# Five places instead of four for softmax probabilities, and inverted denominators written into the attention tile

## The reference, cut to what matters

```python
# L, H, NH, NKV, HD, FF, E, K = (4, 128, 16, 4, 64, 256, 8, 2); 2 rows, 1024 tokens
def _attention(x, wq, wk, wv, wo, cos, sin, causal_bias):
    q, k, v = ...                      # 16 query heads, 4 key/value heads of 64, rotary embedding on q and k
    scores = jnp.einsum('bhqd,bhkd->bhqk', q, k) / jnp.sqrt(jnp.asarray(HD, x.dtype))
    scores = scores + causal_bias
    attn = jax.nn.softmax(scores, axis=-1)
    out = jnp.einsum('bhqk,bhkd->bhqd', attn, v)
    return out.transpose(0, 2, 1, 3).reshape(b, s, NH * HD) @ wo
for l in range(L):
    x = clip(x + _attention(_rms(x, ln1_w[l]), ...), -100, 100)
    x = clip(x + _moe(_rms(x, ln2_w[l]), ...), -100, 100)
```

## Time and profile before

| | |
|---|---|
| runs | 3286.43, 3292.33, 3299.35 us; median 3292.33 |
| profiled execution | 3288.13 us, span of its instructions 3286.3 us |
| granted TensorE clock, mean | 0.98 |
| busy: TensorE, VectorE, ScalarE, GpSimd | 3080.0, 2606.2, 2173.4, 2014.8 us |

### The profile page before, as it was taken

One profiled execution on the slowest core, in us unless ns is written; L12 is line 12 of the kernel. 1 busy time (PEld: TensorE's weight loads), 2 busy tenths in 40 slices (PEclk: granted clock), 3 DMA queues, 4 the chain that ended last, 5 costly groups with the idle time before them and its releaser, 6 DMA issues. The chain is left out here.

```text
span 3286.3 us, 50731 instructions
## 1 busy us (share of the span) xinstructions
PE 3080.0 (94%) x16864; PEld 2042.4 (62%) x16864; DVE 2606.2 (79%) x3764; ACT 2173.4 (66%) x4011; POOL 2014.8 (61%) x1573
## 2 busy tenths in 40 slices
PE   5999999799999999999999999999999999999998
PEld 3555455456666577666665776666657766666576
DVE  6778776678888678888886778888867888888677
ACT  4566667576666676766666767666667676666675
POOL 2100000377878666778776757788767677877675
PEclk8899999899999999999999999999999999999999
DMA  5342421333223055323230653333215532332053
GB/s 121 75 76 49 87 57 38 80 74 81 67 68 75 24 190 146 88 64 77 68 74 16 193 147 83 71 71 76 63 26 190 151 88 66 76 71 66 23 185 112
DMA packets 160401, 283.55 MB, mean 86 GB/s; under 512 B 32592, under 2 KB 64208, under 8 KB 159888
## 3 DMA queue, kind: packets, MB, share of 16 engines
q1 hardware_dynamic: 159632, 280.18, 33.7%
q10 hardware_dynamic: 512, 0.13, 0.0%
HBM read 88.47 MB, written 31.72 MB: 37 GB/s over the span
## 5 line engine op out<-in xcount | busy, mean ns | idle before, releaser
L1473 ACT ACTIVATE prob<-psA 128x512 f32<-128x512 f32 x1152 | 657.6, 593 | 512.0 <-PE psA L1871 329.3
L1275 POOL TENSOR_TENSOR xw<-xw,prob 128x512 f32<-128x512 f32 x672 | 871.9, 1297 | 170.2 <-ACT prob L1473 103.1
L2195 DVE TENSOR_REDUCE mxp<-psA 128x1 f32<-128x512 f32 (+3 forms) x864 | 527.7, 663 | 60.3 <-PE psA L1840 59.6
L2169 DVE RECIPROCAL rden<-psA 128x256 f32<-128x256 f32 x256 | 448.6, 1752 | 151.6 <-PE psA L1899 149.0
L1870 PE MATMUL psA<-qs,ks 128*128 128x512 f32 x1152 | 505.0, 438 | 14.7 <-ACT prob L1473 7.9
L1840 PE MATMUL psA<-ks,qs 128*128 128x512 f32 (+3 forms) x1536 | 439.7, 369 | 40.3 <-DVE ks L2297 16.7
L1275 POOL TENSOR_TENSOR xw<-prob 128x512 f32<-128x512 f32 x224 | 288.2, 1287 | 275.2 <-issue 170.2
L1871 PE MATMUL psA<-qs,ks 128*128 128x512 f32 x1152 | 454.8, 395 | 0.0
L1309 POOL TENSOR_TENSOR hidl<-gate,hidh 128x512 fp32r<-128x512 f32 x256 | 335.5, 1321 | 180.4 <-ACT hidh L1551 178.3
L1485 ACT ACTIVATE psA<-maskq 128x512 f32<-128x512 bf16 (+1 forms) x672 | 359.6, 556 | 83.2 <-DVE mxp L2195 55.7
L2117 DVE TENSOR_REDUCE mxp<-psA 128x1 f32<-128x1024 f32 x256 | 304.7, 1220 | 81.8 <-PE psA L1671 80.9
(11 more groups left out here) (222 smaller groups left out, 5868.5 us busy)
## 6 DMA issues: line engine op xcount, KB each, us to landing
qs<-normed SPq DMA_DIRECT2D x256, 256.0 KB, 4.2
rbp<-rab SPq DMA_DIRECT2D x256, 192.0 KB, 3.4
spread<-routing_weights SPq DMA_DIRECT2D x128, 256.0 KB, 3.6
qs<-qs SPq DMA_DIRECT2D x64, 256.0 KB, 3.9
expert_weight_halves<-eh SPq DMA_DIRECT2D x32, 384.0 KB, 3.7
expert_weight_halves<-el SPq DMA_DIRECT2D x32, 384.0 KB, 4.5
eh<-expert_weight_halves SPq DMA_DIRECT2D x32, 384.0 KB, 3.4
el<-expert_weight_halves SPq DMA_DIRECT2D x32, 384.0 KB, 4.1
```

The source lines that it names most:

```text
L1275: g.tensor_tensor(psum_k[:, t % 2, :], before, prob[:, i % 4, :], ALU.add).then_inc(s_su, 1 if kt > 1 else 2 + (t == 1))
L1473: act(prob[:, k % 4, :], psS[:, k % 2, :], ACT.Exp, scale=float(HD) ** -0.5).then_inc(s_ex, 1)
L2169: vec.reciprocal(rden[:, :], psO[t % 2][:, 256:512]).then_inc(s_rd, 1)
L2195: vec.tensor_reduce(dst, bank, AX.X, ALU.max).then_inc(s_mr, 1)
```

## The change

`prob` gets a fifth place, and the place of a step is its number over all heads and layers modulo 5, instead of its number in the head modulo 4 (36 steps are not a multiple of 5). The semaphores start at 5, and what waits on them asks for one more. The table of the planner names five places too. The tile `rden` is gone: VectorE writes the inverted denominators into `att` and multiplies in place.

```diff
+PLACES = 5
...
-        stage("scalar", ("S", l, n, t, kt), 600, ("tensor", ("S", l, n, t, kt)), back("tensor", "V", 4), back("gpsimd", "S", 4))
+        stage("scalar", ("S", l, n, t, kt), 600, ("tensor", ("S", l, n, t, kt)), back("tensor", "V", PLACES), back("gpsimd", "S", PLACES))
...
-        prob, wst, wvst = over("prob", [P, 4, 512], F32, [("wst", [P, NKV, WG], F32)], [("wvst", [P, NKV * HD], F32)])
+        prob, wst, wvst = over("prob", [P, PLACES, 512], F32, [("wst", [P, NKV, WG], F32)], [("wvst", [P, NKV * HD], F32)])
...
-        rden = sb("rden", [P, 256], where=second)
...
-            g_.sem_inc(s_su, 4)
+            g_.sem_inc(s_su, PLACES)
...
                     if kt == 1:
                         g_.wait_ge(s_dn, it * TPB + t + 1)
-                        before = prob[:, (i - 1) % 4, :]
+                        before = prob[:, (it * TRI[TPB] + i - 1) % PLACES, :]
                     else:
-                        g_.wait_ge(s_su, it * TRI[TPB] + i + 4)
+                        g_.wait_ge(s_su, it * TRI[TPB] + i + PLACES)
                         before = psum_k[:, t % 2, :]
-                    g.tensor_tensor(psum_k[:, t % 2, :], before, prob[:, i % 4, :],
+                    g.tensor_tensor(psum_k[:, t % 2, :], before, prob[:, (it * TRI[TPB] + i) % PLACES, :],
                                     ALU.add).then_inc(s_su, 1 if kt > 1 else 2 + (t == 1))
...
                     if l:
-                        a.wait_ge(s_pv, l * N_ATTN + 4)
+                        a.wait_ge(s_pv, l * N_ATTN + PLACES)
...
-                    act(prob[:, k % 4, :], psS[:, k % 2, :], ACT.Exp, scale=float(HD) ** -0.5).then_inc(s_ex, 1)
+                    act(prob[:, n_ex % PLACES, :], psS[:, k % 2, :], ACT.Exp, scale=float(HD) ** -0.5).then_inc(s_ex, 1)
...
-            t_.sem_inc(s_pv, 4)
+            t_.sem_inc(s_pv, PLACES)
...
-                    ins = mm(psO[t % 2][q * HD:(q + 1) * HD, 0:256], vv[b][:, kt, g * HD:(g + 1) * HD], prob[:, i % 4, q * 256:(q + 1) * 256],
+                    ins = mm(psO[t % 2][q * HD:(q + 1) * HD, 0:256], vv[b][:, kt, g * HD:(g + 1) * HD], prob[:, (it * TRI[TPB] + i) % PLACES, q * 256:(q + 1) * 256],
...
-                total = prob[:, 0, :] if t == 0 else psum_k[:, t % 2, :]
+                total = prob[:, it * TRI[TPB] % PLACES, :] if t == 0 else psum_k[:, t % 2, :]
                 if t != 0:
-                    t_.wait_ge(s_su, it * TRI[TPB] + TRI[t] + t + 5)
+                    t_.wait_ge(s_su, it * TRI[TPB] + TRI[t] + t + 1 + PLACES)
...
                 if t == 0:
-                    v.wait_ge(s_pv, it * TRI[TPB] + 5)
+                    v.wait_ge(s_pv, it * TRI[TPB] + 1 + PLACES)
                 v.wait_ge(s_at, it * TPB + t + 1)
-                vec.reciprocal(rden[:, :], psO[t % 2][:, 256:512]).then_inc(s_rd, 1)
+                vec.reciprocal(att[:, t % 2, :], psO[t % 2][:, 256:512]).then_inc(s_rd, 1)
                 v.wait_ge(s_rd, it * TPB + t + 1)
-                vec.tensor_tensor(att[:, t % 2, :], psO[t % 2][:, 0:256], rden[:, :], ALU.mult).then_inc(s_at, 1)
+                vec.tensor_tensor(att[:, t % 2, :], psO[t % 2][:, 0:256], att[:, t % 2, :], ALU.mult).then_inc(s_at, 1)
```

## The result

The median is 3253.35 us (3250.6 to 3255.82) against 3292.57 of the kernel before (the median over more runs than the 3292.33 shown above): a ratio of 0.9879, 95% interval 0.9863 to 0.9894, or 39 us less. The forecast was 3274. The time lies inside the wide range of 3249 to 3302, 4 us from its lower end, but outside the 3263 to 3283 of the likeliest case, and the gain is more than twice the 18 us that the steps gave. All lines of the changed kernel that are quoted here have numbers one higher than before.

The account below looks back on a forecast made before the run. The prediction took TensorE as the bound, VectorE second. Its terms, 0 + 0 + 11 + 7 = 18 us, gave 3270 from the profiled execution and 3274 from the median; the 8-in-10 range was 3249 to 3302.

Parts of the forecast that it names:

- the likeliest case: The forecast itself for the whole kernel: 3274 us, with its own range of 3263 to 3283; chance 0.52.
- The inverted denominators: VectorE's reciprocals written into the attention tile and multiplied in place: at most 0.5 us either way, taken as 0.
- The semaphore constants: Semaphores start at 5 instead of 4 and readers ask for 1 more: same conditions, no added instruction or DMA, cost 0.
- The fifth place, waits: TensorE's weight loads wait less behind ScalarE as its exponentials' place waits go: 11 us gained, between 0 and 28.
- the rival without change: No measurable change: ScalarE's place waits become waits for scores, gain under 16 us, 3276 to 3295, say 3288; chance 0.27.
- The fifth place, order: New queue order lengthens full runs of value steps on TensorE: 20 runs fewer, 7 us gained, between 0 and 23.
- loads after "issue": Sign on TensorE: full-width weight loads behind a gap ended by nothing the profile shows, taken as run count, fall to about 440.
- the full gain: Rival: waits and order terms both reach their upper bounds, 28 + 23 = 51 us, giving 3241; chance 0.07 (or near it).
- Slower, by maxima held back: Rival: longer narrow runs on TensorE delay VectorE's maxima, 25 us lost, 3317 without the gains; chance 0.14.
- 1752 and 425 ns: Sign on VectorE: the reciprocal and the multiplication of the denominators keep these durations.
- Place waits below 40 us: Sign on ScalarE: waits before exponentials ended by value matmuls and GpSimd sums fall from 105.9 to below 40 us.
- Waits behind exponentials and masks: Sign on TensorE: weight loads' waits for exponentials and masks fall from 134 to about 123 us.

Follow-up runs that it names:

- the four pairs: Four and five places, each with planner's figures as they are, 145 ns, 455 ns and 1510 ns: mean ratios 0.9984 and 0.9883 to the kernel before.

## Why the prediction was right in its range and wrong in its steps

*The inverted denominators* at 0: right, 1.0008 with an interval that holds 1.

*The semaphore constants* at 0: right, the run with five places and the old order, 1.0000, has them in it.

*The fifth place, waits*, at 11 us: wrong, it is 0. The step that failed is "they shrink by the share of place waits in the idle time". With the old order 65 us of the 105.9 went from ScalarE's waits and the loads behind it waited as long as before. For this term the rival without change was right in the outcome, and in its mechanism only in part: it turned all place waits into waits for scores, of which it wanted above 400 us, and they rose by 19 us to 348.3. What the run does show is that the time stays while ScalarE's waits go. That queues whose order was made for four places keep to the pace of four is how I read it.

*The fifth place, order*, at 7 us: the right place with the wrong size. It measured all of the 39 us. I priced only the runs of narrow work. Followed through the trace, there are 443 of them instead of 456, so 13 fewer and not 20, at most 5 us at 0.35. (The count of loads after "issue", which I had named for this, fell to 180 + 121 + 35 + 24 = 360, with 24 from loads of L1907. It was no good measure, since a load that waits for a landing behind a run is counted elsewhere.)

The other 34 us lie elsewhere in TensorE's queue, and the distances from one matmul's start to the next show where. From each distance I take the usual short one for a matmul of its shape (the 20th percentile in the trace). The excess, without that inside the narrow runs, fell from 741.3 us to 702.6 in the whole span, by 38.7. It was 748.2 with five places and the old order, and 704.3 in the run with five places and 1510 ns for the keys. Ahead of a maxima matmul (L1840) that follows full-width work it fell from 80.2 to 49.9 us, ahead of the value steps from 48.7 to 37.7, ahead of the output projections behind full-width work from 26.8 to 17.5. Against this, the excess ahead of the first of two score matmuls (L1870) rose from 100.5 to 113.3, and there stands the new wait for the landings of the maxima's rows. The 30 us ahead of the maxima matmuls fit the waits for masks (21.3 us less on the loads) and for the keys (16.5 us less on the matmuls), but with 1510 ns for the keys and four places the same excess fell to 49.3 us and the kernel became slower: an order moves such waits about, and only their sum counts.

The upper bound of this term was 23 us, so even the bound left the cause out: the step that failed is that the new order was priced by its runs alone, as if everything else in it stayed.

The two errors have opposite signs, 11 us too much and 32 too little. That the time still fell inside the range for 8 in 10 is luck, since the range reached that far for the case of the full gain.

How much of the 39 us is the fifth place and how much a lucky order is told by the four pairs: 33 us on the mean, known to some 26 us either way, and the rest luck of this pair. The fall from three to seven places (1.0058, 1.0000, 0.9879, 0.9833, 0.9792) has the same sign at every step, though each of the other steps is one pair of orders and no larger than the scatter of a pair. That the table's order is the cause of the 39 us is shown by the run that left it out. That its gain comes from the fifth place, and not from any new order, rests on the four pairs and on this fall. Through which waits more places help is open, since the gain lies within the layers from four to five and between them from five to six. Why the step from four to five is the largest is not settled either. By number of runs it should be the smallest, and the kernel before is not an unlucky order (1.0000 against a mean of 0.9984).

*The rivals.* Slower, by maxima held back: VectorE's waits for maxima fell to 49.0 us where this case wanted more than 150, and with the old order in place they were 124.0. That longer full-width stretches ahead of the runs feed VectorE is not shown: with seven places in the table these waits are 97.5 us. The full gain, 3241, was closer than I allowed with 0.07, but through neither of its terms. The Trainium skill (Perfetto Trace Analysis, Identifying Performance Opportunities) says that improving a kernel generally means improving its most-contended engine, and it was borne out in this: ScalarE's waits, taken away alone, gave nothing, and the time went with the distances of TensorE's starts, above.

*What the changed profile was to show.* Seven value steps in a run: yes. 1752 and 425 ns: yes (1753 and 425). Place waits below 40 us: no, 115.4 us for value matmuls alone. Waits behind exponentials and masks down to about 123 us: they fell further, to 101.0, and by the order. Loads after "issue" from 460 to about 440: 360, and no good measure.

## What to carry to other kernels

Where the queues' order is written out ahead of time, a buffer has two effects, and they are to be priced apart: what it frees at run time under the old order, which was nothing here, and what the planner makes of it. The second can't be read from the waits of the old trace, nor from a sum of waits in the new one (134.1 us with four places, 101.0 with five, 134.3 with seven). One pair of orders measures it only to about half a per cent, so move a figure of the planner that should not matter, in both versions, and compare the means. Never mix queues from two plans without timing it: the two queues that do no matmul, exponential or maximum cost 1.3% here when their order alone was changed.

## What the runs showed that was not expected

A nudge of 5 ns in one figure of the planner's table, of 150 or of 460, moved the time by 0.35 and 0.63% with four places, and by 0.36% (slower) and 0.13% with five. The duration that one operation had in the trace of before (1510 ns, for 830 in the table) made the kernel with four places 0.32% slower, while the wait that it was meant to remove did go, and the operation then took 872 ns. A duration read from one order is not that of the next. The planner's figures are no predictor below half a per cent.
